# Two gated cross-attention layers on Trainium2: where the query products of the first four units stand in TensorE's order

## The reference

```
x = x + tanh(g_xattn[0]) * L0_xattn(layernorm(x), ctx)   # 16 heads of 96, 4 key/value heads,
                                                         # keys = 361 of the context + the 100 tokens
x = x + tanh(g_ffn[0])   * L0_ffn(layernorm(x))          # a linear layer and 8 low-rank experts
x = x + tanh(g_xattn[1]) * L1_xattn(layernorm(x), ctx)   # 32 heads of 128, 8 key/value heads,
                                                         # rms norm of each query and key, mask
x = x + tanh(g_ffn[1])   * L1_ffn(layernorm(x))          # stream mixing with Sinkhorn rounds
```

## Time and profile before

| | |
|---|---|
| median of 3 runs | 2566.99 us (2563.04 to 2570.55) |
| the profiled execution | 2567.2 us, span 2565.4 us (1.8 us lie around it) |
| PE busy | 2380.0 us, 93% of the span |
| DVE, ACT, POOL busy | 1479.8, 1077.9, 1047.8 us |
| mean granted TensorE clock | 0.961 of full |
| attention of layer 0, 827 to 1290 us | PE busy 431.01 of 463 us, clock 0.95 |
| attention of layer 1, 1450 to 2400 us | PE busy 921.26 of 950 us, clock 0.99 |

### The profile page before, as it was taken

One profiled execution on the slowest core, in us unless ns is written; L12 is line 12 of the kernel. 1 busy time (PEld: TensorE's weight loads), 2 busy tenths in 40 slices (PEclk: granted clock), 3 DMA queues, 4 the chain that ended last, 5 costly groups with the idle time before them and its releaser, 6 DMA issues. The chain is left out here.

```text
span 2565.4 us, 34613 instructions
## 1 busy us (share of the span) xinstructions
PE 2380.0 (93%) x12916; PEld 2198.7 (86%) x12916; DVE 1479.8 (58%) x2356; ACT 1077.9 (42%) x2453; POOL 1047.8 (41%) x840
## 2 busy tenths in 40 slices
PE   8999999989998899999889789999999999999834
PEld 6888888868998789999788778999999999999833
DVE  7222222233300457778668557888777777777588
ACT  3222222132311466667711245555555555556233
POOL 3000000000000346677664267777776767676130
PEclk9999999999999799999999999999999999999767
DMA  6222222153323322322233223333333333332001
GB/s 201 66 74 70 74 74 62 46 179 107 97 66 97 95 72 84 92 82 77 63 103 99 80 67 100 101 101 100 102 100 108 93 112 94 107 94 82 23 1 52
DMA packets 166093, 224.36 MB, mean 87 GB/s; under 512 B 32346, under 2 KB 126454, under 8 KB 165926
## 3 DMA queue, kind: packets, MB, share of 16 engines
q1 hardware_dynamic: 165926, 222.15, 28.6%
HBM read 183.81 MB, written 38.29 MB: 87 GB/s over the span
## 5 line engine op out<-in xcount | busy, mean ns | idle before, releaser
L1045 POOL TENSOR_TENSOR attend_w_hi<-attend_w_raw,attend_one 128x1024 fp32r<-128x1024 f32 (+1 forms) x178 | 332.7, 1869 | 129.3 <-DMA attend_w_raw<-in_wo 62.9
L1322 DVE TENSOR_TENSOR attend_w_lo<-attend_w_raw,attend_w_hi 128x1024 fp32r<-128x1024 f32 (+1 forms) x182 | 270.5, 1486 | 98.4 <-POOL attend_w_hi L1045 85.2
L1504 PE MATMUL attend_ps_gemm<-normed_hi,attend_w_hi 128*128 128x400 f32 x704 | 247.9, 352 | 17.2 <-DVE attend_w_lo L1312 14.5
L1185 ACT ACTIVATE attend_p<-attend_p,attend_neg_max 100x361 f32<-100x361 f32 x256 | 151.1, 592 | 259.7 <-DVE attend_neg_max L1361 259.7
L1504 PE MATMUL attend_ps_gemm<-attend_o_hi,attend_w_hi 128*128 128x400 f32 x704 | 250.3, 356 | 6.1 <-issue 4.4
L1504 PE MATMUL attend_ps_gemm<-normed_lo,attend_w_hi 128*128 128x400 f32 x704 | 245.5, 349 | 0.0
L1504 PE MATMUL attend_ps_gemm<-normed_hi,attend_w_lo 128*128 128x400 f32 x704 | 244.8, 348 | 0.0
L1504 PE MATMUL attend_ps_gemm<-attend_o_lo,attend_w_hi 128*128 128x400 f32 x704 | 243.1, 345 | 0.0
L1504 PE MATMUL attend_ps_gemm<-attend_o_hi,attend_w_lo 128*128 128x400 f32 x704 | 242.8, 345 | 0.0
L301 DVE TENSOR_TENSOR context_k_square<-context_k_rows 128x512 f32<-128x512 f32 (+1 forms) x46 | 31.8, 692 | 346.6 <-ACT context_k_rows L226 346.5
L1194 ACT ACTIVATE attend_p<-attend_p,attend_exp_inv 100x361 f32<-100x361 f32 (+1 forms) x384 | 208.0, 622 | 0.0
(11 more groups left out here) (306 smaller groups left out, 6380.7 us busy)
## 6 DMA issues: line engine op xcount, KB each, us to landing
attend_w_raw<-in_wq SPq DMA_DIRECT2D x86, 512.0 KB, 3.7
attend_w_raw<-in_wo SPq DMA_DIRECT2D x64, 512.0 KB, 4.3
middle_w_raw<-in_wf SPq DMA_DIRECT2D x25, 512.0 KB, 3.6
attend_w_raw<-in_wo SPq DMA_DIRECT2D x32, 384.0 KB, 3.7
context_ctx_raw<-in_ctxT SPq DMA_DIRECT2D x32, 364.0 KB, 4.9
attend_k_raw<-scratch_k SPq DMA_DIRECT2D x64, 180.5 KB, 3.7
context_ctx_raw<-in_ctxF SPq DMA_DIRECT2D x22, 512.0 KB, 4.6
scratch_v<-context_v_out SPq DMA_DIRECT2D x44, 256.0 KB
```

What stands on the lines that cost most here:

```text
L1045: pool.tensor_tensor(hi, w_flat(w_raw, j % RAW, j), one[:hi.shape[0]].to_broadcast(hi.shape), ALU.mult).then_inc(w_hi_done, 1)
L1185: act.activation(p[:, slot, h], p[:, slot, h], ACT.Exp, bias=neg_max[:, slot, h:h + 1], accum_out=exp_sum[:, slot, h:h + 1]).then_inc(expe ...
L1322: dve.tensor_tensor(w_flat(w_lo, j % SPLIT, j), w_flat(w_raw, j % RAW, j), w_flat(w_hi, j % SPLIT, j).bitcast(F32), ALU.subtract).then_inc ...
L1504: mm = pe.matmul(out, left[a](c), right[b](c), start=(c == 0 and a == b == 0), stop=(c == chunks - 1 and a == 1))
```

## The change

One query tile less is computed in the lead (5 in layer 0, 7 in layer 1), and unit 0 gets that tile in both layers. In units 0 to 3 the query product moves from the end of the unit to the place between `scores(u + 2, 0)` and `turns(u, 2)`; from unit 4 on it stays at the end. The weights of the moved tile are loaded (SP), rounded (POOL) and split (DVE) at new places. `copy_q` on ACT, `remainder_q` on DVE and `squares` on POOL stay at the ends of the units.

```diff
-    LEAD = 2 * QT
+    LEAD = 2 * QT - 1
...
         def query_of(u):
-            if layer == 1:
-                n = u + LEAD - 1 if u else NQ
+            if layer == 1 or u == 0:
+                n = u + LEAD
             elif u % HB == 0:
                 return None
             else:
...
 SP:         tile(LEAD - 1)
-            for j in step_tiles(1):
+            for j in step_tiles(0) + step_tiles(1):
                 tile(j)
...
 POOL:       split_keys(1)
+            for j in query_tiles(0):
+                weights(j)
             for n in range(LEAD - SPLIT + 1, LEAD):
                 squares(n)
...
 DVE:        invert(0)
+            for j in query_tiles(0):
+                split(j)
             maxima(1, 1)
...
 PE:             scores(u + 2, 0)
                 if u >= HB:
                     outputs(u - HB, 0)
+                if u < HB:
+                    queries(query_of(u))
                 if layer == 1:
-                    sum_squares(u + LEAD - 2 if u else NU)
+                    sum_squares(u + LEAD - 1)
                 turns(u, 2)
...
-                queries(query_of(u))
+                if u >= HB:
+                    queries(query_of(u))
```

## The result

The changed kernel takes 2553.68 us (median of 10 runs, 2550.39 to 2559.70), the kernel before 2565.69 in as many (2559.65 to 2574.06). The ratio is 0.9953, 95% interval 0.9942 to 0.9964: 12.0 us or 0.47% faster. The prediction was 2554, range 2546 to 2561, with 12.8 us to be gained. The sum came out. The traces put its two halves elsewhere than the forecast did, layer 0 higher and layer 1 lower; the next sections say how firmly. (In the kernel before, `scores` begins at L1556 and `turns` at L1574, a few lines from where the text before gives them.)

A forecast was written before the change was run, and what follows sets the result against it. In units 0 to 3, PE waits for ACT and DVE mid-unit and they wait for PE at its end. Gains of 7.5 us (layer 0) and 5.3 (layer 1) take 2567.0 to 2554 us, range 2546 to 2561.

The forecast's parts named there:

- PE is not the bound in units 0 to 3, and what is saved there is kept: Both layers: PE has holes in units 0 to 3 and is full from unit 4, so later units only start earlier.
- Layer 0, beats: Layer 0, units 1 to 3: time between starts of `exps(u + 2, 0)` on ACT falls from 15.4 to 11.7 us, gaining 11.1.
- the ring: Units 1 to 3: chain of waits over ACT and DVE, without PE after the move; 11.7 us a unit in layer 0.
- Layer 0, lead and unit 0: Layer 0: lead gains about 0 (4.4 saved, 2.4 stall, 1.8 low clock); unit 0 loses 3.6 us to its added product.
- Layer 1, lead: Layer 1, before unit 0: 2.4 of 4.7 us gained; PE stands some 3 us before `scores(1, 1)`.
- the walk: Layer 1, lead and unit 0 timed step by step: `scores(1, 1)` at 1504.6, unit 1's `exps(3, 0)` starting at 1528.5 us.
- Layer 1, units 1 to 4: Layer 1: units of 12.0, 10.4 and 10.4 us bring unit 4's `exps(6, 0)` to 1561.3 from 1566.63, 5.3 us gained.
- the lock between DVE's split and POOL: Layer 1, units 1 to 3: shared SBUF port blocks DVE's weight split beside POOL; a full block costs 1.5 us a unit.
- The wait for the values: Layer 1, unit 3: PE's wait of 2.70 us for `split_values` goes, as `squares` no longer waits for a late `copy_q`.
- another link: Rival, chance 0.2: POOL's values or squares, or the locked port, leave layer 1 0 to 2 us; 2558 to 2559.5 us.
- PE as the bound: Rival, chance 0.12: ACT and DVE overlap better in units 0 to 3, clock holds; 9 us more, 2545 to 2547.
- A clock that stays low through units 0 to 3: Rival, chance 0.05: PE stays at 1.2 GHz in these units, three cost 28 us; slower, 2582 us.

The follow-up runs named there:

- e8: Changed kernel with `copy_q` and `remainder_q` of the products of units 0 to 3 done a unit later: 2549.48 us, ratio 0.9938.
- e7: Kernel before the change, with only the layer norm steps of layer 1 moved four units later: 2564.84 us, ratio 1.0001.

## Why the prediction was right, point by point

- **PE is not the bound in units 0 to 3, and what is saved there is kept**: right. Behind unit 4 the shift of layer 0 stays between 13.7 and 13.8 us (1.97 of it older than the stage) as far as unit 29.
- **Layer 0, beats**: 11.7 forecast, 11.56 measured, 11.1 us of gain and in the traces 58.0 - 45.9 = 12.2 from the first to the fifth `weigh_values`. That ACT and DVE form the ring was argued then and is shown now by e8.
- **Layer 0, lead and unit 0**: 0 was forecast for the lead and 3.6 us lost for unit 0. The stall of 2.42 us came as said, and so did the lower clock behind it: the 24 matmuls of query 3 took 4.7 to 6.2 us from first to last in the nine profiles with the new lead of layer 0, at a clock of 0.50 to 0.75 in its first 2 us, and 4.2 in the five with the old one. The price was read off a single case: the slow product at 846.91 shows in one of 14 profiles (5.8 us from first to last, after the longest wait there, 2.00 us); in the 13 others it took 4.3, after waits of 0.68 to 1.70 us. It was also read 0.2 us too high, up to ACT's next copy at 853.11; PE's own next product began at 852.91. Lead and unit 0 together, from the first product to the first `weigh_values`, took 50.0 to 52.6 us in five profiles of the new form (mean 51.4) and 48.9 to 50.4 in three of the old (mean 49.7): 1.7 us lost. At the beat of unit 1, for which the 3.6 were forecast, it is 58.9 to 61.5 (mean 60.4) against 57.4 to 59.4 (mean 58.2): 2.2 us lost, not 3.6. This term was oversized, and is the largest part of what brings layer 0 to 10 us in the traces instead of 7.5.
- **Layer 1, lead**: right in kind. `scores(1, 1)` waited 2.28 us, where some 3 were forecast. From the stage's first product to the beat of unit 1 it took 71.41 us for 70.27, so 1.1 us were lost where the walk had 2.6.
- **Layer 1, units 1 to 4**: the step that failed. The ring of 12.0, 10.4 and 10.4 held for two beats (1515.07 to 1526.95 is 11.9, the next 10.5), then the last took 13.0. The forecast named the lock between DVE's split and POOL, priced it at 1.5 us a unit with 0.4 us of air before `o_lo`, and left it in a rival instead of the sum. Two things it did not have: POOL's rounding of the weights comes so late that DVE waits 1.58 us before the split can start, and PE's first output product waits for the `o_lo` behind it. Cost: waits of 1.20 and 3.38 us and a clock of 0.83 in unit 4. At the beat of unit 4 the first profile still had 4.1 of the 5.3 us; to `weigh_values(4)` the means are 2.7, and 1.5 over the whole stage.
- **The wait for the values** in unit 3 of layer 1 went, as said. That it hangs on the late `copy_q` through POOL's squares fits e7, where it stays, but was not tried by itself.
- **Sum**: 7.5 + 5.3 = 12.8 forecast, 10.1 + 2.7 = 12.8 in the traces, 12.0 by the clock. That the number came this close is partly luck: two misses of 2.6 us with opposite signs cancel.
- **Rivals**: another link did hold part of layer 1, and the 1.5 us of the whole stage is in that rival's 0 to 2; what layer 0 gave beyond its forecast hid it in the time. PE as the bound did not come, but was one edit away (e8). A clock that stays low through units 0 to 3 did not come: unit 2 had 1.00.

## What to carry to other kernels

Where PE waits for another engine in the middle of a loop body and that engine waits for PE at its end, put independent matmuls into the first hole; the new length is the larger of PE's own work and the chain over the other engines, and both can be added up from the old trace. Then follow each instruction that the shorter loop brings next to another engine's: what stands behind it in its queue, and who waits for that. A small edit that gave nothing before can pay after such a change: moving the additions gave 6.9 us on the changed kernel and nothing on the old one.

## What the runs showed of the hardware that was not expected

Where a DVE subtraction of two SBUF tiles and a POOL operation met, the later one waited for the other, whichever it was: DVE's split took 2.88 us when POOL had begun 0.08 us before it, and 1.22 when it began 0.03 us ahead of POOL, whose instruction then took 1.91 for 0.86 us. In the lead of layer 0 a wait of PE of 2.4 to 2.5 us was followed by a query product at the lower clock in each of the nine profiles that had it, while the wait of 0.7 to 2.0 us just before query 2 was so only once in 14, the time it was 2.0.
